# Two small steps of a layer norm, on GpSimd or on VectorE

## The reference, cut to what matters

```python
def _layernorm(x, axis=-1, eps=1e-05):
    m = jnp.mean(x, axis=axis, keepdims=True)
    v = jnp.var(x, axis=axis, keepdims=True)
    return (x - m) / jnp.sqrt(v + eps)
...
    x = x + 0.5 * _L0_ffn_ref(_layernorm(x, axis=-1), L0_ffn_router_w, L0_ffn_w1, L0_ffn_w2)
    x = x + _L0_attn_ref(_layernorm(x, axis=-1), L0_attn_W_qkv, L0_attn_W_out)
    x = x + 0.5 * _L0_ffn_ref(_layernorm(x, axis=-1), L0_ffn_router_w, L0_ffn_w1, L0_ffn_w2)
```

## Time and profile before

| | |
|---|---|
| median of 3 runs | 796.1 us (795.56 to 803.17) |
| profiled execution, its own time | 802.07 us |
| its span | 800.3 us |
| mean granted TensorE clock | 0.974 |
| busiest engines by the page | PE 91%, POOL 86%, PEld 74% |
| DVE and ACT | 73% and 75% |

### The profile page before, as it was taken

How to read it: one execution, slowest core, us unless ns; L and a number is a source line. 1 busy time by engine, 2 the same in 40 slices (tenths; PEclk the granted TensorE clock), 3 DMA queues, 4 the chain that set the end, 5 groups by cost and what they waited for, 6 DMA issues and landing times.

```text
span 800.3 us, 13031 instructions
## 1 busy us (share of the span) xinstructions
PE 727.1 (91%) x3600; PEld 590.2 (74%) x3600; DVE 581.4 (73%) x1832; ACT 597.6 (75%) x1219; POOL 686.3 (86%) x668
## 2 busy tenths in 40 slices
PE   1788788889999999999999999999999987979977
PEld 1566566667888888888888888888887866767755
DVE  3456688777879798878778786978686768577533
ACT  3577677658888879888888888797878766656755
POOL 3778867869999999999999999999999858666875
PEclk9999999989999999999999999999999989989999
DMA  5553023023323311322333233322223311303230
GB/s 178 185 162 131 19 88 106 1 106 107 106 107 120 106 76 63 128 82 107 119 107 120 107 121 106 120 89 91 69 100 105 120 50 57 120 2 119 119 120 26
DMA packets 31159, 79.36 MB, mean 99 GB/s; under 512 B 3312, under 2 KB 14448, under 8 KB 31088
## 3 DMA queue, kind: packets, MB, share of 16 engines
q1 hardware_dynamic: 30800, 78.47, 28.7%
q10 hardware_dynamic: 288, 0.07, 0.1%
HBM read 73.81 MB, written 4.72 MB: 98 GB/s over the span
## 4 chain that ended last, share of the span: by engine, by line
PE 32%; DVE 28%; POOL 13%; issue 13%; ACT 10%; DMA 3%; DVEq 1%; POOLq 0%; ACTq 0%; SPq 0%
DVE hid L1033 7%; POOL h_lo L866 6%; PE bank L508 4%; PE bank L528 4%; POOL root_f L860 4%; PE bank L529 4%; PE bank L530 4%; PE bank L510 4%; PE bank L509 4%; ACT h_hi L738 2%; DVE pick_f L1011 2%; PE bank L597 2%; DMA g_all_f<-rows_f 2%; PE bank L489 2%; POOL x_lo_at L854 2%
## 5 line engine op out<-in xcount | busy, mean ns | idle before, releaser
L866 POOL TENSOR_TENSOR h_lo<-hid,h_hi 128x512 fp32r<-128x512 f32 x384 | 492.9, 1308 | 77.0 <-ACT h_hi L738 76.4
L1033 DVE SCALAR_TENSOR_TENSOR hid<-bank,g_all_f 128x512 f32<-128x512 f32 x384 | 262.2, 684 | 141.5 <-PE bank L510 101.1
L727 ACT ACTIVATE hid<-hid 128x512 f32<-128x512 f32 x384 | 228.7, 621 | 51.8 <-DVE hid L1033 51.7
L738 ACT ACTIVATE h_hi<-hid 128x512 fp32r<-128x512 f32 x384 | 225.6, 620 | 4.9 <-PE bank L530 0.4
L508 PE MATMUL bank<-x_hi_f,w_hi 128*128 128x512 f32 x384 | 166.4, 433 | 15.2 <-DVE hid L1033 15.1
L528 PE MATMUL bank<-h_hi,w_hi 128*128 128x512 f32 x384 | 157.4, 410 | 10.8 <-POOL h_lo L866 10.8
L510 PE MATMUL bank<-x_hi_f,w_lo 128*128 128x512 f32 x384 | 154.7, 403 | 0.0
L529 PE MATMUL bank<-h_lo,w_hi 128*128 128x512 f32 x384 | 154.3, 402 | 0.0
L530 PE MATMUL bank<-h_hi,w_lo 128*128 128x512 f32 x384 | 153.8, 400 | 0.0
L509 PE MATMUL bank<-x_lo_f,w_hi 128*128 128x512 f32 x384 | 153.7, 400 | 0.0
L508 PEld LDWEIGHTS bank<-x_hi_f,w_hi 128*128 128x128 f32 x384 | 74.1, 193 | 40.4 <-DVE hid L1033 24.5
(11 more groups left out here) (102 smaller groups left out, 1019.1 us busy)
## 6 DMA issues: line engine op xcount, KB each, us to landing
g_all_f<-rows_f SPq DMA_DIRECT2D x128, 512.0 KB, 5.5
x_sb<-in_x SPq DMA_DIRECT2D x16, 256.0 KB, 3.3
out_x<-x_sb SPq DMA_DIRECT2D x16, 256.0 KB, 7.0
g_all_f<-in_w SPq DMA_DIRECT2D x2, 768.0 KB, 6.7
con<-in_const SPq DMA_DIRECT2D x1, 584.0 KB, 6.2
rows_f<-g_row_f SPq DMA_DIRECT2D x32, 16.0 KB, 1.4
g_all_f<-in_wqkv SPq DMA_DIRECT2D x1, 192.0 KB, 6.4
con<-in_const ACTq DMA_DIRECT2D x1, 68.0 KB, 3.1
```

The source lines that it names most:

```text
L727: fn(h, h, ACT.Square).then_inc(s_sq[s], 1)
L738: fn(h_hi[:, c, :], hid[:, c % STAGE, :], ACT.Copy).then_inc(s_hhi[s], 1)
L866: gp.tensor_tensor(h_lo[:, c, :], hid[:, c % STAGE, :], h_hi[:, c, :].bitcast(F32), ALU.subtract).then_inc(s_hlo[s], 1)
L1033: v.scalar_tensor_tensor(hid[:, c % STAGE, :], hp[c % 2][:], 0.0, g_all[s][:, EXPERT[c], :], ALU.max, ALU.mult).then_inc(s_z[s], 1)
```

## The change

GpSimd no longer makes `ve` and `nm`. VectorE makes both with tensor_scalar instructions directly behind its four bn_aggr, after a wait for them (`s_mv`), and signals `s_ve` once. GpSimd waits for `s_ve` and does the power and the product for the bias. The constant tile `c_eps` and its memset go.

```diff
@@ build
-        c_eps, c_mhalf, c_mone = sb("c_eps", [P, TG]), sb("c_mhalf", [P, TG]), sb("c_mone", [P, TG])
+        c_mhalf, c_mone = sb("c_mhalf", [P, TG]), sb("c_mone", [P, TG])
@@ gpsimd
             gp.memset(router_sb[:], 0.0).then_inc(s_zero, 1)
-            gp.memset(c_eps[:], EPS)
             gp.memset(c_mhalf[:], -0.5)
@@ inv_std
-                pool.wait_ge(s_mv[s], value(n + 1))
-                gp.tensor_tensor(ve[s][:], mv[s][:, :, 1], c_eps[:], ALU.add).then_inc(s_ve[s], 1)
-                gp.tensor_tensor(nm[s][:], mv[s][:, :, 0], c_mone[:], ALU.mult).then_inc(s_ve[s], 1)
-                pool.wait_ge(s_ve[s], value(n * 2 + 2))
+                pool.wait_ge(s_ve[s], value(n + 1))
                 gp.tensor_tensor(rstd[s][:], ve[s][:], c_mhalf[:], ALU.pow).then_inc(s_rstd[s], 1)
@@ mean_variance
                     i = v.bn_aggr(mv[s][:, k, :], bn[s][:, k, :])
                 i.then_inc(s_mv[s], 1)
+                dve.wait_ge(s_mv[s], value(n + 1))
+                v.tensor_scalar(nm[s][:], mv[s][:, :, 0], -1.0, None, ALU.mult)
+                v.tensor_scalar(ve[s][:], mv[s][:, :, 1], EPS, None, ALU.add).then_inc(s_ve[s], 1)
```

## The result

The changed kernel takes 844.08 us (median of six runs, 840.24 to 845.8). The kernel before, run beside it, takes 798.28 us (six runs, 795.56 to 803.17). The ratio is 1.056, with a 95% interval of 1.0532 to 1.0587. The forecast was 818 us in a range of 800 to 831 us, so the sign was right and the size was missed by half: 22 us were expected and 46 were paid.

A forecast was written before the change was run, and what follows sets the result against it. TensorE's and VectorE's parts in series were taken as the bound. 1.1 + 1.4 - 0.25 - 0.2 = 2.05 us, over nine iterations 18 us, plus 4 us at the ends: 22 us on 796.1, 818 us, range 800 to 831.

The forecast's parts named there:

- The bound: Middle iteration: 26.2 us of TensorE plus 17.3 us of VectorE, which has no idle in the second half; GpSimd outside the loop.
- Wait and issue: VectorE's wait for its own bn_aggr and issue of two small instructions: 0.37 us per layer norm, 1.1 us an iteration.
- The slack at `kvm`: At f1, kvm ends before TensorE takes it, so 0.25 us of delay is absorbed in each middle iteration.
- The turn: Each pair on VectorE waits for GpSimd's running instruction, 0.47 us on the mean, 1.4 us in a middle iteration.
- The release of `kf`: VectorE's kf, held by GpSimd's instructions, gets back at most 0.2 us in a middle iteration.
- The ends: Outside the middle: ten places at 0.37 us plus some 0.3 us of turn, less the opening's gain: 4 us.
- No turns: Rival: the pair doesn't take turns with GpSimd and behaves as cwt; 0.65 us an iteration, 804 us, chance 0.2.
- GpSimd as the bound: Rival: GpSimd bounds the middle, so removing its work gains until TensorE caps it; 792 us, chance 0.12.
- Bad phases: Rival: every pair pays the waits of this trace's phases, 3.65 us an iteration; 841 us, chance 0.08.
- The signs: In the trace: nm near 0.5 us median, ve short, period about 45.6 us, longer TensorE waits, GpSimd idle, cwt unchanged.

The follow-up runs named there:

- the pair nowhere: Kernel before with GpSimd's two instructions removed and nothing given to VectorE, so eps and the negation are left out: 804.95 us, ratio 1.0105.
- the earlier statistics: bn_stats and bn_aggr of at moved from around the 17th place to behind the 12th: kernel before 799.31 us (0.9988), changed kernel 831.97 us (1.0372).
- the accumulator form: Changed kernel with both VectorE instructions also writing a sum that nobody reads: 818.76 us, ratio 1.0278.
- on both: Kernel before, GpSimd unchanged, with VectorE making the pair again, also writing sums, into tiles that nobody reads: 817.75 us, ratio 1.0229.
- the three single streams: Kernel before with the change made for one stream only: f1 831.98 us, at 833.42 us, f2 813.29 us.
- f1 alone: Kernel before with the change made for stream f1 only, at and f2 as before: 831.98 us, ratio 1.0394.
- at alone: Kernel before with the change made for stream at only, f1 and f2 as before: 833.42 us, ratio 1.0437.

## Why the prediction was right in sign and wrong in size

**The bound.** Right, with a correction. GpSimd is not in the loop: taking 1.7 us an iteration from it made the kernel 1% slower (the pair nowhere). The loop of TensorE's and VectorE's parts grew by nearly what was put into either. But "in the second half it has none" of idle time doesn't make VectorE the only bound of that half; TensorE is as tight, as the earlier statistics showed.

**Wait and issue.** Taken as 0.37 us a pair, 1.1 in an iteration. f2's pair, which takes no turn, moves the next instruction from 0.29 to 0.54 us behind the start of bn_aggr, so 0.25 us, 0.75 in an iteration. A little too high.

**The slack at `kvm`.** Taken as 0.25 us. Against the L508 that opens TensorE's part, `kvm` ends 1.50 us later (265.81 - 258.54 = 7.27 us before, 277.04 - 268.27 = 8.77 us after) and the `attend` of TensorE starts 1.24 us later (7.58 and 8.82 us), so 0.26 us was absorbed. Right.

**The turn.** This term failed: 1.4 us in an iteration was taken and 2.97 paid, 1.13 at f1 (1.30 us less the 0.17 of the shortest), 1.84 at at (0.68 and 1.16), nothing at f2. That f2's pair would fall under `root_of_weights` was right. The sum has one wait for each pair, of 0.47 us, and no run shows that term. The runs showed in its place a first wait of 1.13 us at f1 and of 0.68 us at at, and a second wait at at, which alone is 1.16 us of each iteration: in the changed kernel `ve_at` took 1.31 to 1.32 us in all nine middle iterations. The timeline of VectorE before already held two rows of this kind, a copy that had waited (it takes 0.42 us otherwise) and an instruction behind it that waited again (it takes 0.21 us at its shortest):

```profile
281.02 0.74 DVE L951 CAST x_hi_f<-xT 128x512 fp32r<-128x512 f32 x1 [2.12 <-ACT xT L696]
281.68 1.30 DVE L1011 TENSOR_TENSOR pick_f<-chosen_f,root_f 128x64 f32<-128x64 f32 x1
```

The second doesn't always wait: with the earlier statistics `ve_at` took 0.16 us in seven of the middle iterations and 1.32 us in two. As for the other 0.4 us, at's first wait is what the phases of the trace had given (0.68 against 0.7), and f1's likewise (1.13 against 1.0); the mean of 0.47 in their place was a choice of mine, and none of the three places paid it.

What the term takes from the kernel before holds in its trace. A waiting instruction lasted until the running `h_lo` ended: 16 of the 32 `cw_f` took 0.37 to 1.15 us and ended 0.02 to 0.03 us behind the end of an `h_lo`, and 12 of the 16 copies to `x_hi_at` took 1.06 to 1.54 us and ended 0.28 to 0.29 us behind one. Under the power (L845) 13 `cw_f` took 0.15 to 0.17 us and nine copies to `x_hi_f` 0.41 to 0.42. And a copy ran at about twice the rate of instructions that read a bank: 512, 256 and 128 columns take 416, 289 and 218 ns at their shortest (L951, L914, L913), which is 0.50 to 0.55 ns for each further column, where tensor_tensor from a bank takes 411 ns for 256 columns (L1084) and 685 for 512 (L1058) in the median, 1.07 ns for each further one.

**What the delay pushes.** Missing from the sum. In the profiled iteration `cw_f` of 306.03 holds the queue 0.47 us longer than at its place before, and `kf` takes 1.07 us (the one of 265.95) instead of 0.91. The release of `kf`, for which 0.2 us was credited, didn't come. These are small beside the turns, but the runs without any turn of the pair (the accumulator form, on VectorE alone and on both) show how large this term can be: their periods grew by 1.9 and 1.3 us, 1.1 and 0.5 beyond the 0.8 of wait and issue.

The balance of an iteration: 0.75 + 2.97 - 0.26 + 0.63 = 4.09 us of the 4.40. Some 0.2 of the remaining 0.3 can be placed, though not explained: f1's bn_aggr starts 0.09 us later behind the L508 (6.54 and 6.63 us), and from the `attend` to the `hid` that ends TensorE's part there are 0.10 us more (18.76 and 18.86).

**The ends.** In the profiled executions 845.8 - 802.07 = 43.7 us, less nine times 4.40, leaves 4 us, as taken. The sum fits, but not as it was made up. By the starts of GpSimd's power for at (205.02, 553.65, 597.22 and 636.39 us before; 206.94, 590.51, 637.16 and 679.45 after) the opening lost 1.9 us, the ninth of the middle iterations and the first closing one 3.1 us each, and everything behind that 0.5 us. Ten places at 0.67 us each aren't seen in this, so that the number agrees is luck in part.

**The rivals.** No turns (804 us): refuted for the plain form, and even the form that has none gives 819. GpSimd as the bound (792 us): refuted. Bad phases (841 us, chance 0.08) gave the right time, and only half by its mechanism. It had three first waits of 2.8 us together; there were two first waits and a second one, 2.97 us. f2's, which it counted with 1.1 us, was nothing. That it comes so near is luck.

**The signs.** As announced: `nm` spreads up to 1.30 us (median 0.64 and 0.85 us, where near 0.5 was expected), waits at L609 for `kvm` appear, GpSimd becomes idle, `cwt` keeps its durations (135 ns in the median, 161 at most). Not as announced: the period (47.95 us, not 45.6), `ve_at`, GpSimd's semaphore (it waits 0.17 us for f1's `ve`), and the wait before the first `hid`, which is 0.58 us where 1 us or more was expected. The lengthening is met earlier, where it arises: 1.03 us at L609 behind f1's pair, and 1.49 us at 303.68, before the first `hid` behind at's.

**Still open.** Why the three single streams cost 80 us together where the whole costs 46 can be read for the most part. Their periods grow by 3.9 (f1), 3.3 (at) and 1.2 us (f2), 8.4 together beside 4.4 for the whole. f1 alone pays a second wait of 1.16 us, which it doesn't in the whole, since GpSimd has nothing left to run, and 1.6 us of lower clock. f2's `nm` alone waits (1.21 us at 254.78 of its kernel), since its pair isn't under the power there. With at alone `kf` takes 1.55 us instead of 1.07. How such meetings fall, and when GpSimd is let in between two VectorE instructions, I can't derive from the traces. No version tried was faster than the kernel before.

## What to carry to other kernels

Before you add a small SBUF-to-SBUF instruction to VectorE, lay its place in the queue over GpSimd's timeline. Here the first of a pair paid up to the rest of GpSimd's running instruction (1.13 us at f1, 0.68 at at) and the second up to a further whole one (1.16 us at at, nothing at f1), so charge both until a trace says otherwise. A form that doesn't wait (here the one with an accumulator, 157 ns) is worth looking for. A queue that is tight beside another one can show no gain when work leaves it (1 us less an iteration, ratio 0.9988) and nearly the full price when work is added. And an engine with idle time isn't free to be made earlier: what it runs then stands elsewhere beside the engine that is the bound (1.7 us less for GpSimd in each iteration, ratio 1.0105).

## What the runs showed of the hardware

- VectorE instructions in a row each waited for a GpSimd instruction of their own, with the earlier statistics from 288.20 us on: 1.29, 1.32 and 1.57 us for three that take 0.17, 0.16 and 0.42 us otherwise. They didn't always: at the same place, in seven of nine iterations, the second took 0.16 us behind a first of 1.26 to 1.28. In the changed kernel every `nm` and `ve` that took more than 0.6 us ended 0.02 to 0.03 us behind the end of an `h_lo`. `ve_at` took 1.32 us in the median beside 128x512 instructions and 0.78 us beside 128x256 ones, but two `nm_at` of 3.49 and 3.48 us lasted through several of the short ones.
- The delay went both ways. In the kernel before, the `h_lo` of 298.73 and the `ve` of 300.25 took 1.56 and 0.65 us with `kf` across both (0.91 us, 0.69 at its shortest), beside some 1.27 us for other `h_lo` and 0.20 us in the median for that `ve` (L842).
- GpSimd's power did not hold these VectorE instructions up. In the changed kernel f2's `nm`, `ve` and `chosen` ran in 0.17, 0.16 and 0.22 us within the 1.63 us of a 128x8 power, and in the kernel before `cw_f` in 0.15 to 0.17 us and the copy to `x_hi_f` in 0.41 to 0.42 within a 128x4 one.
- The form with an accumulator did not wait at any of its 48 places: 150 to 160 ns, where the plain form took up to 1324 ns.
- In the run with f1 alone, the granted clock fell from 1.00 to 0.57 behind an idle time of 2.06 us of TensorE, and the matmuls up to 279.60 started 0.43 us apart instead of 0.23. So it did behind seven of eight idle times of 2.04 to 2.06 us, and not behind the eighth. In the changed kernel it stayed at 1.00 behind idle times of 1.03 and 1.49 us. The fall cost 1.6 us, by both readings above.
